# Start-up of a graph layer on one core: type passes, the scale of M, projections and two rounds of normalising put in another order

## The reference, cut to what matters

```python
h = maximum(layernorm(x), 0)                       # per node, over 384 features
dep_emb = emb[adj]                                 # 45 types, only 0 and 1 occur in adj
hi_t = h_i @ W1[:384] + dep_emb @ W1[384:] + b1
hj_t = h_j @ W2[:384] + dep_emb @ W2[384:] + b2
relevance = sum(hi_t * hj_t, axis=-1)              # 64 x 64 for each graph
A = softmax(where(adj != 0, relevance, -1e9))
h_syn = relu((A @ h) @ gcn_w + gcn_b)
out = x + h_syn @ Wo + bo
```

## Time and profile before

| | |
|---|---|
| three runs | 395.42, 395.7, 395.89 us |
| the profiled execution | 396.95 us, of which the span of its profile is 395.1 us |
| mean granted TensorE clock | 0.965 of full |
| PE | 365.3 us busy (92%) |
| VectorE | 275.7 us (70%) |
| ScalarE | 272.8 us (69%) |
| GpSimd | 193.0 us (49%) |

### The profile page before, as it was taken

How to read it: one execution, slowest core, us unless ns; L and a number is a source line. 1 busy time by engine, 2 the same in 40 slices (tenths; PEclk the granted TensorE clock), 3 DMA queues, 4 the chain that set the end, 5 groups by cost and what they waited for, 6 DMA issues and landing times.

```text
span 395.1 us, 9526 instructions
## 1 busy us (share of the span) xinstructions
PE 365.3 (92%) x3150; PEld 228.7 (58%) x3150; DVE 275.7 (70%) x658; ACT 272.8 (69%) x576; POOL 193.0 (49%) x351
## 2 busy tenths in 40 slices
PE   7942979697999999999999999999999999999986
PEld 7642336463656566665656565656575757565653
DVE  1499765773877777777777685959595858668574
ACT  4212655939688787878787878787969797873833
POOL 2095163283827282837464646556463737291000
PEclk9895898989899999999999999999999999999999
DMA  7970006071838393838375655656565654453143
GB/s 237 349 226 1 0 0 165 2 156 55 189 97 226 80 239 80 239 80 228 90 208 111 186 127 172 128 146 151 153 151 142 161 145 89 117 124 97 66 110 131
DMA packets 82215, 53.87 MB, mean 136 GB/s; under 512 B 45666, under 2 KB 82148, under 8 KB 82196
## 3 DMA queue, kind: packets, MB, share of 16 engines
q1 hardware_dynamic: 81488, 53.22, 50.9%
q0 software_dynamic: 64, 0.20, 0.2%
q10 hardware_dynamic: 644, 0.20, 0.2%
HBM read 17.44 MB, written 12.58 MB: 76 GB/s over the span
## 4 chain that ended last, share of the span: by engine, by line
PE 77%; DVE 8%; issue 5%; POOL 3%; ACT 3%; DMA 2%; ACTq 1%; POOLq 0%; DVEq 0%
PE bank L1025 21%; PE bank L1027 21%; PE bank L1026 21%; PE bank L1110 5%; PE bank L1261 3%; PE bank L1256 3%; DMA x_all<-in_L_gnn_W_b_dram 2%; PE bank L1075 1%; DVE first_sq L685 1%; POOL root_sq L334 1%; DVE first_gap L672 1%; ACT h_tok L464 1%; POOL x_all L413 1%; PE bank L1227 1%; ACT bank L586 1%
## 5 line engine op out<-in xcount | busy, mean ns | idle before, releaser
L407 POOL TENSOR_TENSOR h_parts<-h_tok,h_parts 128x1536 f16<-128x1536 f32 x14 | 43.4, 3099 | 100.3 <-ACT h_parts L455 100.3
L1025 PE MATMUL bank<-gw_hi,hT 128*128 128x385 f16 x192 | 63.6, 331 | 4.3 <-DVE hg_lo L720 2.5
L1027 PE MATMUL bank<-gw_hi,hT 128*128 128x385 f16 x192 | 63.1, 329 | 0.0
L1026 PE MATMUL bank<-gw_lo,hT 128*128 128x385 f16 x192 | 63.1, 329 | 0.0
L1025 PE MATMUL bank<-wo_hi,z_hi 128*128 128x384 f16 x180 | 58.7, 326 | 0.0
L1026 PE MATMUL bank<-wo_lo,z_hi 128*128 128x384 f16 x180 | 58.7, 326 | 0.0
L1027 PE MATMUL bank<-wo_hi,z_lo 128*128 128x384 f16 x180 | 58.7, 326 | 0.0
L1025 PE MATMUL bank<-hT,m_hi 128*128 128x512 f16 x144 | 55.4, 385 | 0.5 <-DVE x_all L919 0.5
L1027 PE MATMUL bank<-hT,m_lo 128*128 128x512 f16 x144 | 55.6, 386 | 0.0
L1026 PE MATMUL bank<-hT,m_hi 128*128 128x512 f16 x144 | 55.4, 385 | 0.0
L413 POOL TENSOR_TENSOR x_all<-x_all,bo_all 128x1536 f32 (+1 forms) x16 | 55.1, 3447 | 0.0
(11 more groups left out here) (150 smaller groups left out, 701.3 us busy)
## 6 DMA issues: line engine op xcount, KB each, us to landing
x_all<-in_x_dram SPq DMA_DIRECT2D x16, 768.0 KB, 6.2
out_dram<-x_all SPq DMA_DIRECT2D x15, 768.0 KB, 4.0
hg_parts<-hg_lo SPq DMA_DIRECT2D x32, 192.0 KB, 3.3
hg_parts<-hg_hi SPq DMA_DIRECT2D x32, 192.0 KB, 3.6
x_all<-in_L_gnn_W_w_dram SPq DMA_DIRECT2D x2, 576.0 KB, 5.2
out_dram<-x_all SPq DMA_DIRECT2D x4, 192.0 KB, 1.9
gcn_raw<-in_L_gnn_gcn_w_dram SPq DMA_DIRECT2D x1, 576.0 KB, 10.4
x_all<-in_L_gnn_Wo_w_dram SPq DMA_DIRECT2D x1, 576.0 KB, 10.9
```

What stands on the lines that cost most here:

```text
L407: nc.gpsimd.tensor_tensor(h_parts[:, :, 1, :], h_tok[:, :, :], h_parts[:, :, 0, :], ALU.subtract).then_inc(h_split, 1)
L1025: nc.tensor.matmul(dst, lh, rh, start=(c == 0), stop=False)
L1026: nc.tensor.matmul(dst, lh, rl, start=False, stop=False)
L1027: last = nc.tensor.matmul(dst, ll, rh, start=False, stop=(c == DC - 1))
```

## The change

Four things are changed; the loop over the supertiles from 3 on keeps its instructions.

1. `types_excess` works in four pieces of 1024 columns with a single-precision result (before: two of 2048, half precision). PE reads the upper half of each word of it. The first two pieces wait until supertile 0 is normalised, the other two for `weight_scales_ready`. Both `make_bias` come behind the coefficients of supertile 1.
2. On PE the first block of M goes ahead of q and p, the second ahead of the bound, and only the third takes the q column. Products with one column are made 64 columns wide (the same column repeated). Two groups of pair products go in front of the early transposes, the others behind them; the six unread matmuls go. On DVE the statistics of supertile 0 come ahead of q and p, and the steps of M's scale stand between steps 8 to 15 of the first coefficients.
3. The third normalise (supertile 2) is shared: ACT makes tiles 0 and 1, DVE tiles 2 and 3 with their low parts (`shared_normalise`), and it has coefficients of its own. POOL makes the coefficients of supertile 3 ahead of `token_low(2)` and `add_bias(0)`.
4. In the second round ACT runs `exponentials(1)` ahead of the fourth normalise. `wo_lo` moves to the first round on DVE, the statistics of supertile 3 ahead of `g_low_part(1, 0)`.

```diff
@@ POOL @@
 def types_excess(n):
-    pool.wait_ge((adj_loaded, adj_rest_loaded)[n], 16)
-    half = adj_all[:, n * HALF:(n + 1) * HALF, :].rearrange("p t j -> p (t j)")
-    nc.gpsimd.tensor_scalar(excess[n], half, -float(EDGE), 0.0, ALU.add, ALU.max).then_inc(type_excess, 1)
+    piece = adj_all.rearrange("p t j -> p (t j)")[:, n * QUARTER:(n + 1) * QUARTER]
+    nc.gpsimd.tensor_scalar(excess[n], piece, -float(EDGE), 0.0, ALU.add, ALU.max).then_inc(type_excess, 1)
...
+pool.wait_ge(h_ready, 2 * KT)
+pool.wait_ge(adj_loaded, 16)
 types_excess(0)
-make_bias(0)
 types_excess(1)
+pool.wait_ge(weight_scales_ready, 1)
+pool.wait_ge(adj_rest_loaded, 16)
+types_excess(2)
+types_excess(3)
 main_coefficients(1)
+make_bias(0)
 make_bias(1)
 main_coefficients(2)
...
+main_coefficients(3)
+token_low(2)
+add_bias(0)
-with pool.Fori(1, LAST - 1) as s:
+with pool.Fori(2, LAST - 1) as s:
@@ ACT @@
-for d in range(DC):
-    m_high_part(d)
+m_high_part(0)
+m_high_part(1)
 early_normalise(0, range(EARLY_WIDE, KT))
+m_high_part(2)
...
 attention_out(1)
-normalise(2, range(1, 2))
 g_high_part(1, 2)
 g_whole(2)
-normalise(2, range(2, KT))
+normalise(2, range(1, ACT_TILES))
 aggregated(1)
 move_scores(1)
-normalise(3, range(0, 2))
 exponentials(1)
-normalise(3, range(2, KT))
+normalise(3)
@@ DVE, first_coefficients @@
+square(0)
+times_var(0)
+dve.wait_ge(bound_wide, 1)
+nc.vector.tensor_scalar(peak[:, SC_M:SC_M + 1], pair_bank[:, BOUND, 0:1], TINY, None, ALU.max)...
+refine(0)
+peak_exponent(SC_M, SC_M + 1, 1)
+square(1)
+scale_from_exponent(SC_M, SC_M + 1, 1)
+times_var(1)
+scale_ready(SC_M, SC_M + 1, 1, m_scale_ready)
+refine(1)
...
@@ DVE, first round @@
-for k in range(DC):
-    rows_and_low(0, k)
+rows_and_low(0, 0)
+dve.wait_ge(wo_high, 1)
+low_part(wo_lo[:, :, :], wo_raw[:, :, :], wo_hi[:, :, :], SC_WO).then_inc(wo_split, 1)
+rows_and_low(0, 1)
+rows_and_low(0, 2)
 statistics(2)
@@ DVE, second round @@
+def shared_normalise(s):
+    dve.wait_ge(early_t, 2 * DC)
+    for k in range(ACT_TILES, KT):
+        mean = third_mean[:, k:k + 1]
+        nc.vector.tensor_scalar(h_tok[:, k, :], x_all[:, s, k, :], mean, mean, ALU.max, ALU.subtract)...
+    dve.wait_ge(coef_ready, COEF_STEPS * (s + 1))
+    for k in range(ACT_TILES, KT):
+        nc.vector.tensor_scalar(h_parts[:, k, 0, :], h_tok[:, k, :], third_mul[:, k:k + 1], None, ALU.mult)...
+    for k in range(ACT_TILES, KT):
+        nc.vector.scalar_tensor_tensor(h_parts[:, k, 1, :], h_tok[:, k, :], third_mul[:, k:k + 1],
+                                       h_parts[:, k, 0, :], ALU.mult, ALU.subtract).then_inc(h_shared, 1)
...
-dve.wait_ge(bias_made, 1)
+dve.wait_ge(bias_made, 2)
 masked_scores(0)
+statistics(3)
 g_low_part(1, 0)
 attention(0, prev=False)
 g_low_part(1, 1)
+third_mean_made()
 attention_high(1, prev2=False)
-low_part(wo_lo[:, :, :], wo_raw[:, :, :], wo_hi[:, :, :], SC_WO).then_inc(wo_split, 1)
 g_low_part(1, 2)
-statistics(3)
+shared_normalise(2)
 aggregated(1)
@@ PE @@
+m_block(0, D)
+... q and p, as before but 64 wide ...
+m_block(1, D)
+... the bound ...
+m_block(2, D + 1)
+... pair products of w1T with pq_cols, two groups ...
+early_transposes(0)
+... pair products of w2T, three groups, and p q ...
-keep_warm(KEEP_WARM, 6)
-early_transposes(0)
```

More of the change, by code:

```diff
@@ L452, in normalise @@
                         act.wait_ge(hT_landed, 16 * (s - 2))
+                mul, add = normal_terms(s)
+                each = KT // ACT_TILES if isinstance(s, int) and s == 2 else 1
                 for k in tiles:
                     for to in (h_tok[:, k, :], h_parts[:, k, 0, :]):
-                        nc.scalar.activation(to, x_all[:, s, k, :], ACT.Relu, bias=ln_add[:, k:k + 1],
-                                             scale=ln_mul[:, k:k + 1]).then_inc(h_ready, 1)
+                        nc.scalar.activation(to, x_all[:, s, k, :], ACT.Relu, bias=add[:, k:k + 1],
+                                             scale=mul[:, k:k + 1]).then_inc(h_ready, each)
             def early_normalise(s, tiles):
@@ L1069, in early_transposes, with spread, m_block @@
                     last.then_inc(early_t, 1)
-            pe.wait_ge(w_copied, 2 * DC)
-            pe.wait_ge(q_copied, 2)
-            for d in range(DC):
+            def spread(column):
+                return column.broadcast_to([column.shape[0], SPREAD])
+            def m_block(d, columns):
                 for c in range(DC):
-                    last = nc.tensor.matmul(bank[d][:, 0:D + 1], w1T[:, c, d * P:(d + 1) * P], w2T[:, c, :],
+                    last = nc.tensor.matmul(bank[d][:, 0:columns], w1T[:, c, d * P:(d + 1) * P], w2T[:, c, 0:columns],
```

194 lines of the change are left out of this document (119 added, 75 removed).

## The result

| | before | after |
|---|---|---|
| median of the runs made together | 395.79 us (395.42 to 396.57) | 383.2 us (382.36 to 383.23) |
| ratio to before | | 0.9674, 95% interval 0.9655 to 0.9694 |
| the profiled execution, its span | 396.95, 395.1 us | 383.2, 381.3 us |
| mean granted clock | 0.965 | 0.982 |
| PE, DVE, ACT, POOL busy | 365.3, 275.7, 272.8, 193.0 us | 361.4, 268.4, 270.2, 192.0 us |

The change gains 12.6 us where 23.6 were forecast; 383.2 lies outside the range.

What follows compares the result with a forecast made beforehand. The chain is 77% PE, which hardly waits from about 97 us, so the time ahead counts. 18.1 + 0 - 0.3 + 4.2 - 0.8 + 1.7 + 0.7 = 23.6 off 395.7 gives 372.1 us; range 368.5 to 375.

Steps and rivals of the forecast that it cites:

- Part 1: Up to the first normalise: DVE's five stalls beside POOL go, bound and coefficients come earlier; gain 18.1 us.
- the ends coincide with the passes: Start: argument that DVE's stalls are POOL's, against the rival of DMA loads (13.1 come back, 385.2 us, chance 0.04).
- Part 2: From the first normalise to the weight scales: faster transposes and clock offset 24 added passes; 0 us.
- Part 3: Type pieces on POOL: 1.0 us each taken, between 0.95 and 3.54, hidden beside supertile 1's statistics; cost 0.
- slow pieces: Rival: the max costs 3.5 us a piece, `gw_lo` and supertile 1 late by 5.2; 377.3 us, chance 0.14.
- Part 4, first round: To the loop: `wo_lo` ahead of two `rows_and_low` delays type flag and supertile 1's transposes by 0.3 us.
- beside it runs `token_low(2)`; I charge half of that, 0.8: Second round: `shared_normalise` on DVE beside POOL's `token_low(2)`; contention cost 0.8 us, bounds 0 and 1.55.
- Part 4, the rest: Second round: last hg tile 1.1 us earlier, third g chunk's wait of 2.9 gone; 4.2 in all.
- the clock: Second round: stretch at 0.83 gone, 1.7 us; half of two stretches at 0.50, 0.7 us.
- The loop: Later supertiles: instructions kept, bound by PE; no gain or loss, 0.
- makes DVE the last instead of ACT: Rival: the shared third normalise makes DVE last, so the second round gives nothing; 377.2 us, chance 0.11.

Runs made afterwards that it cites:

- e7: Kernel before plus one wait: POOL's first excess pass held until supertile 0 is normalised; 396.02 us, ratio 0.9979.
- e13: Kernel before with its excess passes multiplying by one instead of taking the max, still half precision, no clamp; 387.09 us, ratio 0.9763.
- e1: Changed kernel with the four excess pieces multiplying by 1 instead of taking the max with 0, no clamp; 377.87 us, ratio 0.9526.
- e5: Changed kernel with four kinds of piece: multiply or max, each to half or single precision; one run, 377.75 us.
- e2: Changed kernel with POOL waiting for both shared tiles of the third normalise ahead of `token_low(2)`; 375.61 us, ratio 0.9478.
- e4: Changed kernel with both multiplying pieces (no clamp) and POOL held until the shared normalise is done; 371.4 us, ratio 0.9375.
- e14: Changed kernel, POOL held until the shared normalise is done, last two pieces on ACT as Relu, its new column behind all tiles; 371.94 us, ratio 0.9374.
- e8: Changed kernel with two tiles of the fourth normalise put back ahead of `exponentials(1)`; 382.29 us, ratio 0.9651.
- e9: Changed kernel with POOL's `token_low(2)` held only until the two products of `shared_normalise` are made; one run, 377.43 us.

## Why the prediction was wrong, step by step

- **Part 1 (18.1): right in size and cause.** The transposes of supertile 0 start 17.3 earlier, and 0.64 of the rest is that the weights were copied at 10.23 instead of 9.59 in this execution. That DVE's stalls were POOL's is shown by e7 and e13: they move with POOL's passes and shorten with them. One argument for it was too strong, that "the ends coincide with the passes": three of the five do, but `first_gap` and the `first_sq` of 4.35 us ended 2.6 ahead of theirs (23.67 by 26.23, 32.81 by 35.38).
- **Part 2 (0): right.** From the early transposes to the statistics of supertile 1 it is 8.02 us, 7.91 before, at full clock and with 24 more passes in it.
- **Part 3 (0): the failed step.** "I take 1.0": it is 3.6. The value lay at the upper bound, just above its 3.54, and the choice fell to the lower one: the row weighed against the result type, `token_low`, spoke for the max, and I still took the price of the pass without it. e1 and e5 show the max alone. The rival "slow pieces" had the cause and nearly the price (5.2; 5.3 in e1, 4.2 from e2 to e4), but half of the wrong way: `gw_lo` was not held. The cost ran through POOL's queue. Pieces 2 and 3 take 5.1 more (7.21 by 2.06). From the statistics to the transposes it is 17.37 us instead of e1's 14.59, so 2.8 of it showed; the other 2.3, by the difference, lay where e1 waits for the branch. The half clock behind the wait adds 1.2 (transposes to last hg tile 19.21 in e2, 17.97 in e4).
- **Part 4, first round (-0.3): right.** From the statistics to the transposes 14.58 in e4, 14.39 before.
- **Part 4, "beside it runs `token_low(2)`; I charge half of that, 0.8" (bounds 0 to 1.55): the other failed step.** The stall was 4.55, three times the upper bound. It was bounded by `token_low` alone; but the second product, stalled in turn, lasted until POOL's next pass, `add_bias` (3.53), was through. What was missing in the bound is the queue of the engine beside it. With the half clock behind the 6.44 us wait, another 2.4.
- **Part 4, the rest (4.2), and the clock (2.4): near in sum, wrong in the split and in one cause.** Once both waits are short, the stage from supertile 1's transposes to supertile 2's scores gains 7.6 in e4 and 7.2 in e14, where 5.8 were forecast. All stretches of half clock went; I had counted half of two, and the two too low: "they cost 1.4 together", but 3 us at 0.50 are 1.5 for the first alone. The granted clock before was 0.61 and 0.66 in 59.4 to 62 and 62 to 64, 0.61 and 0.54 in 80 to 82 and 82 to 84, and 0.57 in 97 to 101, which makes 5.1 us lost (an estimate: each length times what the clock lacked); in e4 it is 1.00 from 41.8 to 82. So the clock gave some 5.1 of the 7.6 and the shorter waits some 2.5, where 2.4 and 4.2 were counted. The exponentials' order, credited with part of this, gives nothing (e8).
- **The loop (0): right.** From the scores of supertile 2 to the end 287.7 before, 287.4 after.
- **The rivals and the range.** Two rivals came true at once: slow pieces (5.2), and the shared third normalise that "makes DVE the last instead of ACT", so that "the second round gives nothing" (5.1). Together they give 372.1 + 5.2 + 5.1 = 382.4, and 383.2 was measured; the range had room for one of them at a time. The second came true by a cause that it did not name: in e2 the sharing is the same, only POOL waits, and from supertile 1's transposes to supertile 2's scores it gains 6.4 (41.59 by 47.96).

The Trainium skill (GPSIMD Engine Reference, Key points) names contention on SBUF interfaces that GpSimd shares with VectorE, for two SBUF inputs or a two-port mode. The runs agree for the subtractions (e9: 2.52 instead of 1.14). They do not for `gw_lo`, which has two SBUF inputs and kept its 1.66 beside a piece in the changed kernel. The products that stalled for 4.55 have one tensor input; whether they run in a two-port mode no run here shows. I had used the rule for the 0.8; the sign was right, the length was not.

## What to carry to other kernels

The price of a POOL pass hangs on its operations, not on its size alone: where two rows of like shape differ by a factor of three, a different operation in the slow one is the first suspect, and replacing one word is the cheapest experiment there is. When DVE has to work beside POOL, bound the stall by everything that stands in POOL's queue there, and try DVE's PSUM work in that place (`z_lo` kept its length there); a wait that only moves POOL moved the stalls along (e7). When two rivals concern different stages, add their prices before closing the range. A long wait of PE costs more than its length: the half clock behind the two here added 1.2 and 2.4 us.
